# A transformer block on one core: column tiles of 32 for the second half of the attention output, sums of four key tiles on GpSimd, another order of issues on SyncE

## The reference, cut to what matters

```
x = x + Attention(layernorm(x))     # 16 heads of 32, rotary Q and K, causal softmax, output projection Wo, bo
x = x + FFN(layernorm(x))           # silu(x Wg^T gs) * (x Wu^T us), 1408 wide, then Wd and ds
```

## Time and profile before

| | |
|---|---|
| median of 3 runs | 750.68 us (748.65 to 753.9) |
| profiled execution | 749.88 us, its span 748.2 us, granted clock 0.999 |
| PE busy | 732.0 us, 98% |
| DVE, ACT, POOL busy | 443.8 us (59%), 310.9 us (42%), 247.7 us (33%) |

### The profile page before, as it was taken

How to read it: one execution, slowest core, us unless ns; L and a number is a source line. 1 busy time by engine, 2 the same in 40 slices (tenths; PEclk the granted TensorE clock), 3 DMA queues, 4 the chain that set the end, 5 groups by cost and what they waited for, 6 DMA issues and landing times.

```text
span 748.2 us, 10633 instructions
## 1 busy us (share of the span) xinstructions
PE 732.0 (98%) x3563; PEld 539.3 (72%) x3563; DVE 443.8 (59%) x1071; ACT 310.9 (42%) x641; POOL 247.7 (33%) x224
## 2 busy tenths in 40 slices
PE   8999999999999999999999999999999999999996
PEld 7887888766656666666666548788788888888885
DVE  6978684897778787777878545853243125114113
ACT  3322231266666666666666662222332232222221
POOL 0816152411114242333324245822232223223223
PEclk9999999999999999999999999999999999999999
DMA  8686469635576667676667356540001001001001
GB/s 280 230 284 232 162 254 309 255 115 160 162 192 172 185 172 194 168 188 164 187 162 187 102 185 225 222 201 1 0 20 38 0 1 56 0 0 56 1 1 59
DMA packets 54318, 104.39 MB, mean 140 GB/s; under 512 B 14820, under 2 KB 18404, under 8 KB 53748
## 3 DMA queue, kind: packets, MB, share of 16 engines
q1 hardware_dynamic: 54264, 103.72, 44.0%
HBM read 69.62 MB, written 38.21 MB: 144 GB/s over the span
## 4 chain that ended last, share of the span: by engine, by line
PE 81%; DVE 6%; issue 5%; DMA 3%; POOL 2%; ACT 1%; SPq 1%; DVEq 0%; POOLq 0%; ACTq 0%
PE ps L1105 32%; PE ps L1244 18%; PE ps L1130 10%; PE ps L1223 10%; PE ps L1320 9%; DMA x_st<-in_x 1%; PE ps L1097 1%; POOL hid_lo L592 1%; DVE xn L786 1%; DVE stats L771 1%; DMA rec_l<-rec_rows 1%; DMA w_st<-in_wk 1%; DMA l_cols<-o_raw 1%; ACT p L683 0%; DVE esin L893 0%
## 5 line engine op out<-in xcount | busy, mean ns | idle before, releaser
L683 ACT ACTIVATE p<-ps 128x384 f32<-128x384 f32 (+3 forms) x384 | 162.0, 489 | 58.0 <-PE ps L1223 57.8
L843 DVE CUSTOM_DVE_ANT_0 masked<-ps,mask_qk 128x512 bf16<-128x512 f32 (+1 forms) x240 | 113.2, 500 | 56.6 <-PE ps L1130 55.7
L1244 PE MATMUL ps<-p,v_slot 128*64 128x512 f32 (+3 forms) x768 | 137.3, 494 | 0.2 <-ACT o_raw L690 0.2
L1223 PE MATMUL ps<-q_st,k_st 99*128 99x384 f32 (+2 forms) x384 | 135.7, 361 | 1.1 <-ACT p L683 1.0
L1056 DVE SCALAR_TENSOR_TENSOR hid<-ps,us_sb,silu 128x512 f32<-128x512 f32 x44 | 33.0, 751 | 165.2 <-PE ps L1105 159.5
L1130 PE MATMUL ps<-k_st,q_st 96*128 96x512 f32 (+2 forms) x384 | 128.9, 357 | 2.0 <-DVE row_max L843 1.7
L592 POOL TENSOR_TENSOR hid_lo<-hid,hid_hi 128x512 fp32r<-128x512 f32 x44 | 56.8, 1290 | 173.0 <-ACT hid_hi L758 173.0
L561 POOL TENSOR_SCALAR_AFFINE_SELECT p<-p 128x512 f32<-128x512 f32 x64 | 40.6, 635 | 209.0 <-ACT p L683 209.0
L1244 PEld LDWEIGHTS ps<-p,v_slot 128*64 128x64 f32 x768 | 50.1, 136 | 74.2 <-issue 62.2
L1130 PEld LDWEIGHTS ps<-k_st,q_st 96*128 96x128 f32 x384 | 72.3, 189 | 29.7 <-DVE row_max L843 14.3
L1223 PEld LDWEIGHTS ps<-q_st,k_st 99*128 99x128 f32 x384 | 72.1, 189 | 16.9 <-issue 6.3
(11 more groups left out here) (117 smaller groups left out, 1080.8 us busy)
## 6 DMA issues: line engine op xcount, KB each, us to landing
qk_scratch<-st_hi SPq DMA_DIRECT2D x32, 512.0 KB, 3.6
q_st<-qk_scratch SPq DMA_DIRECT2D x32, 384.0 KB, 3.8
k_st<-qk_scratch SPq DMA_DIRECT2D x32, 384.0 KB, 4.8
flag_st<-in_ffn SPq DMA_DIRECT2D x32, 264.0 KB, 2.8
ffn_copy<-in_ffn SPq DMA_DIRECT2D x32, 264.0 KB, 3.5
qk_scratch<-st_lo SPq DMA_DIRECT2D x16, 512.0 KB, 3.7
o_T<-o_raw SPq DMA_DIRECT2D x32, 128.0 KB, 4.2
rec_l<-rec_rows SPq DMA_DIRECT2D x32, 128.0 KB, 3.3
```

The costliest lines, as they stand in the source:

```text
L683: act.activation(p32[:, at:at + q0 + w - keep], ps[:, ST_BANK + i % ST_RING, keep - q0:w], ACT.Exp, scale=SCALE).then_inc(exp_done, 1)
L843: ins = dve.tensor_tensor_reduce((masked_a if u < 2 else masked)[:, s_before(i) % 2, col:col + kept], scores, mask_qk[:, 512 - kept:512], ...
L1223: pe.matmul(ps[:, ST_BANK + i % ST_RING, 0:w], k_st[0:K_ALL, slot, kt * P:(kt + 1) * P], q_st[0:K_ALL, slot, q0:q0 + w], start=True, stop= ...
L1244: ins = pe.matmul(ps[VW * a:VW * (a + 1), o_bank(u, half), q0 - 512 * half:512], v_slot[:, slot, kt, :], p32[:, at:at + n], start=(kt == 0 ...
```

## The change

Pair 15 aside, queries 512 to 1023 are now done in two parts of 256 (`part` 1 and 2; part 0 is queries 0 to 511, as before, with all 64 columns). In parts 1 and 2 PE's columns are cut into four tiles of 32: for each head one takes V alone (`"v"`), the other takes in turn the ones (`"l"`, for the sums) and V of one or two further key tiles (`"w"`), whose output goes into columns 256 to 511 of the bank and is added on POOL later (`o_joined`). The sums of key tiles 0 to 3 are one product, because POOL first adds the four tiles of exponentials (`sum_p`, three tensor_tensor of 128x512 for each head up to head 29). Pair 15 (`PV_TAIL`) keeps 64 columns, three parts in three banks, no sums.

- ACT evacuates three parts for a pair, SP moves six DMAs for a pair instead of four (`o_w` is new), all counted by `o_moved`.
- SP: `load_max` stands ahead of `move_pair` and `store_rec` in each step.
- `test_weights` does its piece in two halves, one waiting for the other (`flag_bits` has half the size).
- `wo_st` is loaded in step 30 and not in stage A. `bo_sb` and `ds_sb` are issued ahead of the moves of pair 14; POOL adds the bias of chunk 0 before it scales group 6, and of chunk 1 before the last group, which is scaled in two halves of queries. `load_rec` of group 6 writes into `k_st`.

```diff
+PV_GROUPS = [
+    (0, [[("vl", 0)], [("vl", 1)], [("vl", 2)], [("vl", 3)]]),
+    (1, [[("v", 0), ("w", 4)], [("v", 1), ("l", None)], [("v", 2), ("l", 4)], [("v", 3), ("l", 5)], [("w", 5)]]),
+    (2, [[("v", 0), ("w", 6)], [("v", 1), ("l", None)], [("v", 2), ("l", 4)]]),
+    (2, [[("v", 3), ("l", 5)], [("v", 4), ("l", 6)], [("v", 5), ("l", 7)], [("w", 7)]]),
+]
...
             def output_products(u, group):
+                part, rounds = (PV_TAIL if u == PAIRS - 1 else PV_GROUPS)[group]
...
+                elif group == 1:
+                    if u < PAIRS - 1:
+                        pe.wait_ge(p_summed, 2 * u + 2)
                     pe.wait_ge(p_high_masked, 2 * u + 2)
...
+                for products in rounds:
                     for a in range(2):
+                        for kind, kt in products:
+                            output_product(u, a, part, kind, kt)
...
             def move_pair(u):
-                sp.wait_ge(o_evac, 2 * u + 2)
+                sp.wait_ge(o_evac, PARTS * (u + 1))
...
+                    sp.dma_start(o_w[t // 4 % 2][rows, :], o_raw[l_rows, u % 2, S:S + 2 * QW]).then_inc(o_moved[u % 2], 16)
...
             def b_step(t):      # SP
+                if t + 1 < HEADS:
+                    load_max(t + 1)
                 if t % 2 == 0 and t >= 4:
                     move_pair((t - 4) // 2)
                 if t % 4 == 3 and t >= 7:
                     store_rec((t - 7) // 4)
-                if t + 1 < HEADS:
-                    load_max(t + 1)
...
-            move_pair(PAIRS - 2)
-            sp.wait_ge(pv_half[1], PAIRS)
+            sp.wait_ge(pv_part[2], part_done(2, PAIRS - 1))
             sp.dma_start(bo_sb[:, :], bo.partition_broadcast(P)).then_inc(c_in, 16)
             sp.dma_start(ds_sb[:, :], ds.partition_broadcast(P)).then_inc(c_in, 16)
+            move_pair(PAIRS - 2)
...
+            def sum_p(t):       # POOL
...
+                pool.tensor_tensor(total, second_half(0), second_half(1), ALU.add).then_inc(p_sum_step, 1)
+                pool.wait_ge(p_sum_step, 2 * t + 1)
+                pool.tensor_tensor(total, total, second_half(2), ALU.add).then_inc(p_sum_step, 1)
+                pool.wait_ge(p_sum_step, 2 * t + 2)
+                pool.tensor_tensor(total, total, second_half(3), ALU.add).then_inc(p_summed, 1)
...
             for t in range(HEADS):
                 copy_v(t)
                 if t % 4 == 0 and t >= 8:
                     scale_group((t - 8) // 4)
-                mask_p(t)
-            scale_group(GROUPS - 2)
+                mask_low(t)
+                if t < HEADS - 2:
+                    sum_p(t)
+                mask_high(t)
...
             add_bias(0)
-            scale_group(GROUPS - 1)
+            scale_group(GROUPS - 2)
             add_bias(1)
+            scale_last_group()
...
             def reciprocals(g):     # DVE
                 for k in range(2):
-                    dve.wait_ge(o_moved[k], 64 * (g + 1))
+                    dve.wait_ge(o_moved[k], 96 * (g + 1) - (32 if (g, k) == (GROUPS - 1, 1) else 0))
```

More of the change, by code:

```diff
@@ L96, with part_done @@
 TEST_AFTER = (4, 4)
[L97 to L101, removed]
+PV_GROUPS = [
[4 rows of a table added]
+]
+PV_TAIL = [
+    PV_GROUPS[0],
+    (1, [[("vl", kt)] for kt in range(6)]),
+    (2, [[("vl", kt)] for kt in range(4)]),
+    (2, [[("vl", kt)] for kt in range(4, 8)]),
+]
+assert len(PV_GROUPS) == len(PV_TAIL) == len(PV_AFTER[0]) + len(PV_AFTER[1])
+PV_FIRST = {("vl", 0, 0), ("vl", 1, 0), ("vl", 2, 0), ("v", 1, 0), ("w", 1, 4), ("v", 2, 0), ("w", 2, 6)}
+PV_LAST = {("vl", 0, 3), ("vl", 1, 5), ("vl", 2, 7), ("v", 1, 3), ("l", 1, 5), ("w", 1, 5), ("v", 2, 5), ("l", 2, 7), ("w", 2, 7)}
+PARTS = 3
+PART_DONE = (2, 4, 4)
+QW = 256
+def part_done(part, pairs):
+    return PART_DONE[part] * pairs if part == 0 or pairs < PAIRS else PART_DONE[part] * (PAIRS - 1) + 2
+SUM_KT = KT // 2
+SUM_SLOTS = 3
 FFN_COLS = KC * INTER
@@ L159, in transformer_block @@
             xst_c = sb("xst_c", [P, TJ, H], F32, after_wo)
-        wo_st = sb("wo_st", [P, KC, H], F32)
+        p_sum = sb("p_sum", [P, SUM_SLOTS, S // 2], F32)
+        o_w = [sb(f"o_w{k}", [P, S // 2], F32) for k in range(2)]
         with ExitStack() as after_v:
@@ L180, in transformer_block @@
         q_st = sb("q_st", [P, SLOTS, S], F32R)
+        with ExitStack() as after_two_k:
+            wo_st = sb("wo_st", [P, KC, H], F32, after_two_k)
         with ExitStack() as after_k:
@@ L273, in transformer_block @@
         p_high_masked = sem("p_high_masked")
-        pv_half = [sem(f"pv_half{k}") for k in range(2)]
+        p_sum_step = sem("p_sum_step")
+        p_summed = sem("p_summed")
+        p_sum_read = sem("p_sum_read")
+        pv_part = [sem(f"pv_part{k}") for k in range(PARTS)]
         o_evac = sem("o_evac")
@@ L469, in b_step @@
                     load_head(t + SLOTS, t % SLOTS)
+                if t == HEADS - 2:
+                    sp.wait_ge(st_ps, NPC * t)
+                    sp.dma_start(wo_st[:, :, :], wo).then_inc(wo_in, 16)
             load_max(0)
@@ L558, in mask_p, with mask_high @@
+            def mask_high(t):
+                base = t % SLOTS * P_SIZE
                 high = p32[:, base + P:base + P + KT // 2 * S].rearrange("p (j w) -> p j w", w=S)[:, :, S - P:S]
[L559 to L562, removed]
+                pool.wait_ge(exp_done, NPC * (t + 1))
+                pool.affine_select(out=high, in_=high, compare_op=ALU.is_ge, fill=0.0, base=0,
+                                   pattern=[[0, KT // 2], [1, P]], channel_multiplier=-1).then_inc(p_high_masked, 1)
@@ L734, in _ @@
                 o_hi(0, j)
[L735 removed]
+            evacuate(PAIRS - 1, 1)
+            evacuate(PAIRS - 1, 2)
             for c in range(N_CH):
```

167 lines of the change are left out of this document (117 added, 50 removed).

## The result

The changed kernel takes 767.12 us (median of five runs, 763.38 to 774.74); the kernel before, on the same chip, 749.69 us (748.65 to 753.9). The ratio is 1.0226, with an interval from 1.0189 to 1.0264: slower by about 17 us, where 745 was forecast. The profiled execution of after has a span of 761.7 us, 13.5 longer than that of before. It is also the shortest of the five, and what follows explains the 13.5. Its granted clock was 0.989, and that of the execution of 767.12 us 0.984: 0.005 of 762 us, 3.8 us as an estimate, is about what lies between the two (3.7). Of all runs told of here one, the longest of e10 (748.73 us), counts as slow and is not in its ratio.

What follows compares the result with a forecast made beforehand. PE was taken to bound stage B. Output groups -19.8, evacuation +0.6, weight tests +6.9, moves +6.0 and passage +1.0 summed to -5.3 us: 744.6 against the profiled 749.88, forecast as 745 for the median; range 731 to 758.

Steps and rivals of the forecast that it cites:

- the passage from B to C: POOL's biases and scaling before PE's chunk 2: between -1.2 and +4.5 us, taken as +1.0.
- have to land 6.9 us sooner to make up: Passage: POOL's 22.7 us row starting at 453.83 would reach 478.3 unless the output biases land 6.9 us sooner.
- They are issued 8 us sooner: Passage: bias loads issued 8 us sooner, after pair 14's last group, but behind two x loads and wo_st.
- In step 30 DVE has no scores: Reason to charge DVE's wait for the moves, 1.0 us each, in steps 6, 10, ..., 26 but not 30.
- The output groups: Stage B on PE: four streams side by side save 1.32 us a pair, -19.8 us over 15 pairs (-13.2 if tied).
- rivals 2 and 4: 2: streams tied by rounds, -13.2 instead of -19.8, 752, chance 0.13; 4: only two streams overlap, +46 us, 796, chance 0.05.
- The split alone, 0.2 us, fits the gaps: DVE's weight test in two halves: the extra 0.2 us was expected to cost nothing.
- The moves: Six moves behind the rows of maxima delay DVE's reciprocals; PE loses 1.0 us in six steps, +6.0 (4.3 to 7.3).
- rival 1: The new waits on DVE and POOL cost little: -16 us, 734, or 730 with moves free too; chance 0.22.
- The weight test: DVE's test halves held by POOL's sums after scaled steps: 1.15 us in six steps, +6.9 (0 to +13.8).
- rival 3: POOL bounds the weight test in all 15 odd steps: +18.8 us, in all +6.6, 757 to 762; chance 0.10.
- ACT's +0.6: Third evacuation for each pair: nothing, except 0.6 us once in steps 30 and 31, where no scores cover it.

Runs made afterwards that it cites:

- e10: Changed kernel with the passage from B to C rearranged, weight tests after scaled steps moved a step earlier, and SP's order chosen by step; 743.8 us, ratio 0.9889.
- e5: Changed kernel with loads of wo_st and x issued later, bo and ds ahead of x, and group 6 scaled before chunk 0's bias; 756.0 us, ratio 1.0065.
- e8: Changed kernel with the old SP order, load_max behind move_pair and store_rec in all steps; 759.6 us, ratio 1.0119.
- e1: Changed kernel with DVE's reciprocals of steps 6, 10, ... taken after piece 2 of the next step instead of after piece 10; 761.8 us, ratio 1.0147.
- e11: Changed kernel with load_max behind move_pair and store_rec only in steps with t % 4 of 2 or 3; 759.5 us, ratio 1.0145.
- e12: The kernel before with one part of the change alone, load_max first on SP; 751.3 us, ratio 1.0012.
- e6: e1 plus the weight test of steps 9, 13, ..., 29 taken one step earlier, its piece issued ahead of the moves; 755.8 us, ratio 1.0068.
- e9: Changed kernel with the second and third addition of each POOL sum on 16 columns instead of 512; 762.4 us, ratio 1.0132.
- e2: Changed kernel with the weight test as a tensor_scalar reading one SBUF input instead of two; 763.8 us, ratio 1.0140.

## Why the prediction was wrong

- **The step that failed is the passage from B to C.** The text put it "Between -1.2 and +4.5, I take +1.0"; it measured +9.1 to chunk 2 and +11.4 to the end, and e5, which rearranges only this passage, is 11 us below the changed kernel. The chain of work on POOL was right: 22.5 us from `ds_sb` to the first half of the last scaling (458.17 to 480.7), 22.7 in the text. Its start was not. The biases "have to land 6.9 us sooner to make up", and +1.0 takes 5.9 of that as given. Counted from group 0 of pair 14 they landed 2.2 us later than before (31.3 us behind it instead of 29.1), and 6.9 + 2.2 is the 9.1. "They are issued 8 us sooner" rested on what releases the issue: it came to 4.0, counted in the same way. The two loads of x and `wo_st` were named, but the landing behind them (11.3 us) had no price of its own, and the store of group 6, which stands ahead on SP, was left out. That store was issued 9.2 us behind group 0 of pair 14 instead of 3.2, late by DVE's wait for moves (5.8 us in step 30; with moves first, e8, it is 4.9), and took 6.7 us to land behind `wo_st`. "In step 30 DVE has no scores" was true and irrelevant: the late reciprocals cost there by way of SP.
- **The output groups were right.** 1.43 us instead of 2.09 twice for each pair: 1.31 of the 1.32 forecast, so rivals 2 and 4 are out. Of that a pair without other waits keeps 1.1 (17.1 against 18.22; e8, e10). The missing 0.2, about 3 us over 14 pairs, is for the most part DVE with no slack left between groups 2 and 3: in e8's pair this stretch is 0.52 us shorter and not 0.66, DVE goes from the test into the maxima without a gap, and PE's score bank at 183.44 follows DVE's release at 183.40. "The split alone, 0.2 us, fits the gaps" had that at nothing.
- **The moves were right in place and size.** The six pairs with reciprocals are 6.7 us longer than six of 17.1 (109.3 - 102.6), +6.0 forecast; e1 takes 4.8 of it back in these pairs, e8 and e11 6.0. The sum counted the order and six moves; the sentence against rival 1 put the wait down to the order alone, and e12 shows that it takes both.
- **The weight test was right in place, somewhat small in size.** The six pairs with a test after a scaled step are 8.1 us longer (110.7 - 102.6), forecast +6.9 (0 to +13.8); e6 takes 3.9 of it back in these pairs. e9 shows the sums in some 5 us of PE's waits, e6 that the bias holds the test as well. In plain steps the halves take 0.43 us each, so rival 3 failed at its place, though its time was the nearest.
- **What no step had:** the clock. In the changed kernel it cost 1.6 us at chunk 2 and 1.7 at the entry into B, behind a wait of 1.10 us for DVE (the clock was 0.57 from 168 to 172 us); worked out from stretches of 1 us, busy time times one less the clock.
- So the fourteen pairs add up: 14 x 17.1 is 15.6 less than before, +6.7, +8.1 and +1.6 for the first two (one waits 0.9 us for `k_st`) make +0.8, as measured, where the forecast's terms gave them -5.6. Of the 18.8 us between the forecast's -5.3 and the 13.5 found, 11.1 are the passage (where the forecast's +1.0, ACT's +0.6 and the 1.3 of the fifteenth pair make +0.3), 6.4 the pairs and 1.3 the entry into B. Rival 1, the waits costing little, is the opposite of what happened, and the time lies beyond every rival but the fourth, whose mechanism did not happen. One sum is wrong as well: the upper end of 757 leaves tied streams out, though the text counts them in; with them it is 13.0 above before, 764, and the 767 lie above that too.

## What to carry to other kernels

A load that is moved to where it is needed is to be costed by what then stands behind it, on the issuing queue and in the transfers: here 1 MB of weights ahead of a store of 16 KB, and 2 MB ahead of two biases, turned a free engine's idle time into 10 us of the bound engine's. Where an edit makes the bound engine faster, work out first how much slack each helper has at each place (bank by bank), since all small waits of the helpers come onto the path at once. And parts of a change that lose are worth separating from the part that gains: the four streams shortened their groups by what was promised, and 23 us lay in four places of order around them.

## What the runs showed of the hardware

- Products on four tiles of 32 columns, from two heads, ran side by side: eight records of 256 columns (four products of two passes) in 0.64 us (252.84 in the changed kernel). They were not tied by rounds: group 1 took 1.87 us and group 3 1.44, where the prediction gives 2.1 and 1.65 for tied streams.

```profile
252.84 0.64 PE L1352 MATMUL ps<-p,v_slot 128*32 128x256 f32 x8
```

- The weight test on DVE, whose operands are in SBUF, was held by POOL with two inputs and with one (e2), and beside a sum, a bias (which let it go about 1.4 us after it began) and a mask; a half beside a mask took 0.745 us, and that mask 0.83 instead of 0.63 (e6). Maxima read from PSUM kept their 0.68 us beside the same sums.
- The granted clock fell to 0.50 behind single waits of PE of about 1.1 to 2.3 us and stayed there for some 3 to 7 us (e8: 231.53 above), but not behind each one (in the changed kernel a wait of 1.66 us at 275.37 left it at 1.00), and in e12 it fell at the entry into B with no wait over 0.6 us near. By stretches of 1 us the loss was 3.3 us in the changed kernel's profiled execution, 12.6 in e8's and none in that of before. What decides it stays open, and with it most of the spread between executions of one kernel.
